# Cross-attention on one core: the products of the context one half slot earlier, the transposes of the values behind them, ScalarE's work in TensorE's order

## The reference, cut to what matters

```
q = heads(x @ to_q_w)
for rows, wk, wv in four segments of ctx:            # 77, 4, 4, 43 rows
    out += softmax(q @ heads(rows @ wk).T / 4) @ heads(rows @ wv)
y = out @ to_out_w + to_out_b + x
```

## Time and profile before

| | us |
|---|---|
| median of 3 runs | 1683.23 |
| lowest, highest | 1682.04, 1683.94 |
| the profiled execution, its own time | 1681.79 |
| its span, first to last instruction | 1679.6 |
| TensorE busy | 1571.8 (94%) |
| GpSimd busy | 1448.2 (86%) |
| VectorE busy | 1399.0 (83%) |
| ScalarE busy | 1271.1 (76%) |
| SyncE's transfers, share of 16 DMA engines | 85.6% |

### The profile page before, as it was taken

The page is one execution under the profiler, slowest core; times in us unless marked ns, Lnnn a source line. Parts: engine busy times, 40 slices in busy tenths (PEclk is TensorE's granted clock), DMA queues, the critical chain, the costliest instruction groups (busy, mean ns, idle before and its releaser), DMA issues.

```text
span 1679.6 us, 51529 instructions
## 1 busy us (share of the span) xinstructions
PE 1571.8 (94%) x16252; PEld 1416.0 (84%) x16252; DVE 1399.0 (83%) x3359; ACT 1271.1 (76%) x2416; POOL 1448.2 (86%) x1646
## 2 busy tenths in 40 slices
PE   6879999999999999999999999999999999999976
PEld 3568888899888889888888988888898888899865
DVE  3358888988888898888888888889888888988896
ACT  1247888887887887788788778878877888887765
POOL 3459899989989999998998998999899899989865
PEclk9989999999999999999999999999999999999999
DMA  8688989988988988898898889899889989988961
GB/s 308 175 219 197 217 233 243 216 217 220 240 211 228 250 197 232 217 242 211 234 239 205 231 215 231 221 239 231 209 227 223 219 230 242 216 219 224 218 143 34
DMA packets 423237, 366.26 MB, mean 218 GB/s; under 512 B 19041, under 2 KB 394274, under 8 KB 418850
## 3 DMA queue, kind: packets, MB, share of 16 engines
q1 hardware_dynamic: 423202, 365.80, 85.6%
HBM read 216.38 MB, written 149.34 MB: 218 GB/s over the span
## 4 chain that ended last, share of the span: by engine, by line
PE 76%; ACT 10%; issue 7%; DVE 3%; POOL 1%; DMA 1%; SPq 1%; ACTq 1%; POOLq 0%
PE job_ps L934 16%; PE ring_ps L1012 13%; PE ring_ps L1035 10%; PE ring_ps L1025 10%; PE job_ps L921 9%; PE s_ps L985 6%; PE job_ps L960 5%; ACT probs L644 3%; ACT pT L656 2%; PE ring_ps L885 2%; PE job_ps L963 2%; ACT v_new L602 1%; PE job_ps L944 1%; DVE l_seg L797 1%; ACT c L624 1%
## 5 line engine op out<-in xcount | busy, mean ns | idle before, releaser
L526 POOL TENSOR_TENSOR probs<-probs,rl 128x616 f32<-128x616 f32 (+1 forms) x640 | 629.2, 1005 | 65.7 <-DVE rl L808 65.3
L797 DVE TENSOR_REDUCE l_seg<-probs 128x8 f32<-128x616 f32 (+1 forms) x640 | 386.5, 646 | 137.2 <-ACT probs L644 137.1
L656 ACT ACTIVATE pT<-ring_ps 128x512 f32<-128x512 f32 x640 | 373.4, 603 | 164.2 <-PE ring_ps L1012 160.1
L1012 PE MATMUL ring_ps<-ident,probs 128*128 128x128 f32 x2560 | 389.6, 277 | 11.2 <-DVE y_all L819 8.7
L770 DVE TENSOR_TENSOR probs<-s_ps,m_seg 128x616 f32<-128x616 f32 (+1 forms) x640 | 387.8, 649 | 0.0
L754 DVE TENSOR_REDUCE m_seg<-s_ps 128x8 f32<-128x616 f32 (+1 forms) x640 | 371.5, 623 | 3.5 <-issue 0.2
L644 ACT ACTIVATE probs<-probs 128x1024 f32<-128x1024 f32 x320 | 341.3, 1067 | 7.9 <-DVE probs L774 7.9
L1012 PEld LDWEIGHTS ring_ps<-ident,probs 128*128 128x128 f32 x2560 | 290.1, 143 | 44.7 <-issue 25.0
L934 PE MATMUL job_ps<-c,w 128*128 128x312 f32 x1860 | 304.7, 313 | 0.9 <-POOL c L507 0.9
L934 PEld LDWEIGHTS job_ps<-c,w 128*128 128x128 f32 x1860 | 272.5, 190 | 1.3 <-POOL c L507 1.3
L1035 PE MATMUL ring_ps<-w_o,oT 128*128 128x320 f32 x1152 | 202.6, 320 | 47.5 <-ACT pT L656 45.1
(11 more groups left out here) (69 smaller groups left out, 2047.9 us busy)
## 6 DMA issues: line engine op xcount, KB each, us to landing
q_all<-q_scratch SPq DMA_DIRECT2D x64, 960.0 KB, 7.9
k_all<-k_scratch SPq DMA_DIRECT2D x64, 960.0 KB, 12.3
c_in<-in_cT SPq DMA_DIRECT2D x32, 1024.0 KB, 5.7
x_raw<-in_xT SPq DMA_DIRECT2D x32, 768.0 KB, 7.2
q_scratch<-parts SPq DMA_DIRECT2D x64, 384.0 KB, 4.7
k_scratch<-parts SPq DMA_DIRECT2D x64, 384.0 KB, 5.5
x_res<-in_x SPq DMA_DIRECT2D x128, 160.0 KB, 3.5
out<-y_all SPq DMA_DIRECT2D x128, 160.0 KB, 3.3
```

Source lines behind the costliest of these rows:

```text
L526: pool.tensor_tensor(pr[:, :, a:e], pr[:, :, a:e], r[:, :, s:s + 1].broadcast_to((P, OH, e - a)), ALU.mult)
L656: act.activation(pT[:, h:h + QH, :], ring_ps[i][:, :].rearrange("p (h s) -> p h s", h=QH), ACT.Copy)\
L797: dve.tensor_reduce(l_seg[:, o % 2, :, s:s + 1], pr[:, :, a:e], axis=AX.X, op=ALU.add)
L1012: last = pe.transpose(ring_ps[i][:, k * S:(k + 1) * S], probs[:, (o % NR) * OH + q * QH + k, :], ident[:, :])
```

## The change

`SEQ` and `PIECES` put job `kv` 0 wholly into slot 6 (before, it began at the end of slot 6 and ended in slot 7), `v` 2 into slot 7, `kv` 1 from the end of slot 7 to the middle of slot 8 and `v` 3 behind it. `c_high` 0 moves from slot 5 to 4, `c_low` 1 from slot 6 to 5. For splits that end at place 1, GpSimd's `make_rest` and `make_third` and ScalarE's `round_second` come one slot sooner. In the slots with a projection (1, 3, 6, 8), ScalarE copies the first transposition before it evacuates and rounds, and in every slot it evacuates a job that ended at place 0 before the copy of the second transposition. SyncE issues the context's load before the second of the two key stores at the body's start.

```diff
-SEQ = [("kv", 3), ("kv", 4), ("q", 0), ("v", 0), ("q", 1), ("v", 1), ("q", 2), ("v", 2), ("kv", 0), ("v", 3),
-       ("kv", 1), ("kv", 2)]
+SEQ = [("kv", 3), ("kv", 4), ("q", 0), ("v", 0), ("q", 1), ("v", 1), ("q", 2), ("kv", 0), ("v", 2), ("kv", 1),
+       ("v", 3), ("kv", 2)]
...
-          (6, 0, ("v", 2), None), (6, 1, ("kv", 0), 0), (7, 0, ("kv", 0), 1), (7, 1, ("v", 3), None),
-          (8, 0, ("kv", 1), 0), (8, 1, ("kv", 1), 1), (9, 0, ("kv", 2), 0), (9, 1, ("kv", 2), 1)]
+          (6, 0, ("kv", 0), 0), (6, 1, ("kv", 0), 1), (7, 0, ("v", 2), None), (7, 1, ("kv", 1), 0),
+          (8, 0, ("kv", 1), 1), (8, 1, ("v", 3), None), (9, 0, ("kv", 2), 0), (9, 1, ("kv", 2), 1)]
...
-CHI_AT, CLO_AT = [5, 5], [5, 6]
+CHI_AT, CLO_AT = [4, 5], [5, 5]
...
                 if live(g + 1, G):
                     store_parts(g + 1, 4)
-                    store_parts(g + 1, 5)
-                finish(g, -2)
                 if live(g + 2, G):
                     load_c(g + 2)
                     load_small(g + 2)
+                if live(g + 1, G):
+                    store_parts(g + 1, 5)
+                finish(g, -2)
...
-                    for turn, job in ended(g, n - 2 - at, at):
+                    for turn, job in ended(g, n - 2, at):
                         if job in SPLITS:
                             make_third(turn + 2, SPLITS.index(job))
...
-                    for turn, job in ended(g, n - 1 - at, at):
+                    for turn, job in ended(g, n - 1, at):
                         if job in SPLITS:
                             make_rest(turn + 2, SPLITS.index(job))
...
+            def free_banks(g, n):
+
                 for turn, job in ended(g, n - 1, 1):
                     evacuate(turn, job)
                 for at in range(2):
-                    for turn, job in ended(g, n - 2 - at, at):
+                    for turn, job in ended(g, n - 2, at):
                         if job in SPLITS:
                             round_second(turn + 2, SPLITS.index(job))
...
+                if n not in PROJECT_AT:
+                    free_banks(g, n)
...
-                    if kind == "tr" and what[1] == 0 and n in VALUES_AT and live(g * NB + VALUES_AT[n], B):
-                        oT_high(g * NB + VALUES_AT[n])
-                for turn, job in ended(g, n, 0):
-                    evacuate(turn, job)
+                    if kind == "tr" and what[1] == 0:
+                        if n in PROJECT_AT:
+                            free_banks(g, n)
+                        if n in VALUES_AT and live(g * NB + VALUES_AT[n], B):
+                            oT_high(g * NB + VALUES_AT[n])
+                        for turn, job in ended(g, n, 0):
+                            evacuate(turn, job)
```

More of the change, by code:

```diff
@@ L707, in _ @@
             act.activation(w_o[0][:, :, :], wo_raw[:, :, :], ACT.Copy).then_inc(wo_hi_made, 1)
+            def free_banks(g, n):
+                for turn, job in ended(g, n - 1, 1):
+                    evacuate(turn, job)
+                for at in range(2):
+                    for turn, job in ended(g, n - 2, at):
+                        if job in SPLITS:
+                            round_second(turn + 2, SPLITS.index(job))
             def slot(g, n):
@@ L712, in slot @@
                     exponent(g, n)
-                for turn, job in ended(g, n - 1, 1):
-                    evacuate(turn, job)
-                for at in range(2):
-                    for turn, job in ended(g, n - 2 - at, at):
-                        if job in SPLITS:
-                            round_second(turn + 2, SPLITS.index(job))
+                if n not in PROJECT_AT:
+                    free_banks(g, n)
                 for at, (nn, kind, what) in enumerate(FILLS):
```

## The result

| | before | after |
|---|---|---|
| median, us | 1683.59 | 1669.17 |
| lowest, highest | 1682.04, 1686.96 | 1658.82, 1671.05 |
| the profiled execution, its own time | 1681.79 | 1671.05 |
| its span | 1679.6 | 1668.8 |
| TensorE busy | 1571.8 (94%) | 1571.7 (94%) |

The ratio is 0.9899, with the interval 0.9855 to 0.9943: faster, by 14.4 us, where 38 were forecast. The time lies within the range, near its upper end. The runs of the kernel after lie 12 us apart, those of the kernel before 5. The four runs of the kernel after stand in the order of their mean granted clock: 1671.05 us (the profiled one) at 0.986, 1670.74 at 0.988, 1667.60 at 0.989, 1658.82 at 0.993.

The account below looks back on a forecast made before the run. TensorE was taken to set the pace, 46.8 us per group without its waits. 30 x (2.5 - 1.1 - 0.1) = 39 us off and 0.7 on gave 1643.5 profiled, a median of 1645, range 1615 to 1678.

Parts of the forecast that it names:

- Slots 6 and 8: TensorE's waits of both slots' projections and of `kv` 1 in slot 8 vanish: 2.5 us less per group.
- VectorE, GpSimd: GpSimd's slot 5 work ends at 823.9, before `kv` 0's second half at 824.27: no wait, 0.3 us to spare.
- D: Rival: GpSimd becomes the bound in slot 5, TensorE waits 0.2 us there; 1645 to 1650; chance 0.55 together with forecast and E.
- Slot 7: the new wait: TensorE's second transposition waits for ScalarE, whose evacuation of `kv` 0 waits on (a) and (b): 1.1 us per group.
- (a): Slot 7, ScalarE's evacuation of `kv` 0 needs `q` 1's third part, at 827.3; alone a 0.3 to 0.4 us wait.
- (b): Slot 7, ScalarE's evacuation of `kv` 0 needs `q` 0's stores landed, at 828.5, 14.7 us after the stacks' load starts.
- It waits 1.0 us; I take 1.1: Size of TensorE's wait in slot 7, from ScalarE done at 829.9 and the transposition due at 828.9.
- Before the loop: `kv` 2's bank now follows `kv` 1's instead of `v` 3's: up to 0.7 us more, once.
- B: Rival: `q` 0's stores land later, slot 7's wait is 2.1 us, 9 us are left, 1674; chance 0.17.
- C: Rival: `q` 0's stores land after 830.0, slot 7's wait is 3.0 us, slower at 1701; chance 0.08.
- A: Rival: `q` 0's stores land in time, only (a) remains in slot 7, 63 us off, 1620; chance 0.2.
- E: Rival: ScalarE's order changes nothing; slot 6's remaining 0.5 us comes off slot 7's wait; 1646; chance 0.55 with forecast and D.

Follow-up runs that it names:

- e6: e1 with GpSimd making the third part of `q` 1 before the scaling of octet 5 in slot 6: 1613.69 us.
- e8: e1 with ScalarE's old order put back: 1636.34 us, ratio 0.9715 to the kernel before.
- e1: The kernel after with SyncE's context load put back behind the key store of split 5 and the output: 1622.49 us.
- e7: The kernel after with SyncE's load of `x` (768 KB) moved ahead of the stores of `q` 0: 1777.20 us.
- e3: The kernel after with 40 unused identity products on TensorE once before the loop, while it waits for the context: 1665.01 us.
- e10: The kernel before with only remainders, third parts and second roundings of splits ending at place 1 made one slot sooner: 1695.93 us.
- e4: The kernel after with ScalarE's old order put back: 1665.58 us, ratio 0.9882 to the kernel before.

## Why the prediction was wrong in size and right in mechanism

**What bounds the kernel, and the 46.8 us of a group without waits.** Right: e6 reaches 46.9 with TensorE busy in 1299.67 of 1300 us.

**Slots 6 and 8, 2.5 us per group.** Right: the waits are gone, and slot 6's projection comes 1.96 us after the slot's first transposition, 1.97 forecast. e8 shows that ScalarE's order had a share of only 0.44 us in it while the jobs stand as in the change.

**Slot 0, "0 to 0.1 us".** Right: the weight load waits 0.23 us there, none of it in the matmuls' record, and the group without other waits (e6) is 0.1 longer than the 46.8.

**VectorE, GpSimd.** Right: in the group shown `c_low` is ready at 816.63 and `kv` 0's second half begins at 816.92, 0.3 us later as foreseen, and it waits for `c_low` in no group of the loop. D did not come.

**Slot 7: the new wait, its place and its chain.** Right. Stacks 6.4 us after the context forecast, 6.5 in the group shown; 14.7 us from there to the landing forecast, 14.7 to L616. Both conditions were there, (a) at 0.3 us as e1 and e6 show, (b) above it. TensorE's wait was forecast at 1.0 us; the 1.00 of this group's matmul record is not that number. By the prediction's own four steps (2.80 us from the scores at 818.78) the transposition was due at 821.58 and began 1.16 us later, and the weight load was idle 1.24 us.

**"It waits 1.0 us; I take 1.1": the term that failed first.** It was worked out from single rows, and these were among the early ones: the context's landing from the low half of 4.9 to 5.7 us, the 14.7 us from one group. Over the 29 groups of the kernel after, the stacks start 6.75 us after the context's issue in the mean (6.31 to 7.27), and L616 follows 14.83 us later (14.28 to 15.37). That is 21.58 us where 6.4 + 14.7 = 21.1 was taken. The weight load's idle time in slot 7, the prediction's measure of a wait, has a mean of 1.53 us in the 25 undisturbed groups (0.99 to 1.95) where 1.1 was taken. The terms give 49.28 - 2.5 + 1.1 + 0.1 = 47.98 us for a group, and the 25 have a mean of 48.4: the 0.42 us are this term. Over 29 groups they cost 12 us.

**What no term stood for: the clock.** The prediction read that the clock was full in the steady part and left it there. There no projection waited longer than 1.5 us. The new wait reaches 2.09 us in the matmuls' record, behind the four longest (1.86 and more) the clock fell, and these groups take 2.3 us more each: 9 us in the profiled execution. With the 12 us above this is the 21.6 us by which the loop missed (16.1 won; 29 x 1.3 = 37.7 forecast). e7 shows the clock taking as much again as the delay itself. The steady part of before could not price such a term, and e3 shows that waits of this length do not always bring it.

**Before the loop "up to 0.7 us more": 3.6 in this execution.** `kv` 2's bank cost 0.16 us. The rest is the clock that stayed at half behind TensorE's longest gap, and e7 and e10 show that this comes and goes whatever the place of `v` 2 (to the third query job e7 takes 127.3 us, the kernel before 129.2, e10 131.0). What the change itself costs there is open.

**The last two groups, nothing: 1.7.** There the wait in slot 7 came once at 3.43 us, and the clock is 0.91 from 1600 to 1640 us, where it was 1.00; 1.7 us is the sum, not parted further.

**The rivals.** The result lies between the forecast and B (1674), by B's place and for a reason of its size, later landings, plus one that B didn't have. C's mechanism is real, as e7 shows, but the context's place alone was not enough for it. A is what e1 gives without that part, 1622.49 where 1620 was worked out for a wait by (a) alone. E's arithmetic is borne out by e4 (with the old order on ScalarE the time is the same), but E was not what happened: with the new order the waits are gone.

**What the sum should have asked.** Each part was costed as it stands in the whole, which gave the right mechanism. That one part, the context's place, made the wait that ate 47 of the 61 us which the others bring (1622.49 against 1683.2) was there to be read: the prediction priced A at 1620 and named the context as the cause of the difference.

## What to carry to other kernels

A load moved forward in an in-order queue is also a load put in front of every store behind it. Before it is moved, follow the first store that lands behind it to whoever waits for its buffer, and price the wait from the mean and the late tail of the landings over all groups, not from one row. A wait that ends with a landing makes each gain ahead of it worthless and each loss free, so test a part with that wait and without it before it is called useless. And where a wait of TensorE grows beyond those that the trace has at full clock, the sum needs a term for the clock behind it, or at least a wider range on the slow side.

## What was not expected of the hardware

Behind waits of 1.86 to 2.09 us in a stream that else keeps TensorE busy the granted clock fell to 0.50 for a few microseconds, four times in 29 groups. In e3 six waits of 1.87 to 1.99 us passed without a fall, and so did the 3.43 us of the kernel after's last group (the clock is 1.00 from 1556 to 1600 us). What decides is open; no run here tells it apart. Behind the longer waits of e7 (2.73 to 4.28 us) the mean clock from 200 to 1500 us was 0.96.

The first of the small transfers behind the loads of the stacks holds SyncE's queue for 5.1 us (808.27 in the group shown), and by this the queue's own time is a part of the 14.8 us from the stacks' start to the landing. Whether a second queue for the stacks would free the stores was not tried.
